# First and last batch of a fused attention and expert layer: filler turns, later weights, four output banks

## The reference

```
xn  = layernorm(x)
q, k, v = split(xn @ wqkv);  q, k = relu(q), relu(k);   16 heads of 16
kv  = cumsum(k[:, None] * v[None, :]);  y = (q . kv) / (q . cumsum(k) + 1e-5)
attention = y @ wo
scores = sigmoid(xn @ Wr);  the two best of 8 by scores + bias;  cw = their scores, normed
hid[e] = silu(xn @ Wg[e]) * (xn @ Wu[e]);  routed = sum over e < 4 of cw[e] * (hid[e] @ Wd[e])
routed += (cw[4] + cw[6]) * xn + cw[7] * relu(xn)
conv   = causal depthwise convolution of xn over 4 rows, + conv_b
out = x + attention + routed + conv
```

## Time and profile before

| | us |
|---|---|
| median of 3 runs | 1334.67 (1334.45 to 1334.83) |
| profiled execution, time | 1334.1 |
| its span, first to last instruction | 1332.3 |
| TensorE busy | 1312.0 |
| VectorE busy | 1120.6 |
| GpSimd busy | 822.7 |
| ScalarE busy | 737.4 |

### The profile page before, as it was taken

How to read it: one execution, slowest core, us unless ns; L and a number is a source line. 1 busy time by engine, 2 the same in 40 slices (tenths; PEclk the granted TensorE clock), 3 DMA queues, 4 the chain that set the end, 5 groups by cost and what they waited for, 6 DMA issues and landing times.

```text
span 1332.3 us, 54753 instructions
## 1 busy us (share of the span) xinstructions
PE 1312.0 (98%) x24384; PEld 1136.9 (85%) x24384; DVE 1120.6 (84%) x2574; ACT 737.4 (55%) x1543; POOL 822.7 (62%) x673
## 2 busy tenths in 40 slices
PE   5999999999999999999999999999999999999998
PEld 4888888888888888888888888888888888888887
DVE  7988889888898888898888988888888889888885
ACT  5645566545556455565555564556645655545561
POOL 2676566675575755666656757556666566575554
PEclk9999999999999999999999999999999999999999
DMA  5011211111211111111111011111111111111110
GB/s 181 30 39 66 66 53 47 35 66 66 66 34 50 51 66 65 50 50 35 66 66 65 35 49 51 66 66 50 50 34 67 66 65 35 35 65 50 51 49 18
DMA packets 46828, 73.73 MB, mean 55 GB/s; under 512 B 6529, under 2 KB 42241, under 8 KB 42497
## 3 DMA queue, kind: packets, MB, share of 16 engines
q1 hardware_dynamic: 45888, 69.23, 15.2%
q10 hardware_dynamic: 704, 1.01, 0.2%
HBM read 53.18 MB, written 17.04 MB: 53 GB/s over the span
## 4 chain that ended last, share of the span: by engine, by line
PE 97%; DVE 1%; POOL 0%; ACT 0%; DMA 0%; issue 0%; POOLq 0%; DVEq 0%
PE ring L303 51%; PE scores L303 17%; PE ring L423 7%; PE ring L439 6%; PE scores L372 5%; PE state_sum L386 4%; PE ring L459 2%; PE scores L312 2%; PE scores L354 2%; DMA x_t<-in_L_attn_x_dram 0%; DVE cT L828 0%; ACT qp L548 0%; DVE sm L807 0%; PE scores L321 0%; POOL hid L687 0%
## 5 line engine op out<-in xcount | busy, mean ns | idle before, releaser
L687 POOL TENSOR_TENSOR hid<-hid,cwb 128x512 f32<-128x512 f32 x128 | 172.0, 1343 | 225.4 <-DVE hid L836 224.7
L828 DVE SCALAR_TENSOR_TENSOR cT<-xT,conv_ws,cT 128x512 f32<-128x512 f32 x192 | 292.3, 1561 | 0.0
L675 POOL TENSOR_TENSOR x_t<-x_t,same 128x1024 f32<-128x1024 f32 x32 | 76.9, 2404 | 242.7 <-ACT same L557 242.7
L814 DVE TENSOR_TENSOR state_bd<-state_sum,tables_s 128x256 f32<-128x256 f32 x248 | 103.7, 418 | 135.9 <-PE state_sum L386 135.8
L578 ACT ACTIVATE sg<-ring 128x512 f32<-128x512 f32 x128 | 76.8, 600 | 251.3 <-PE ring L303 251.3
L303 PE MATMUL ring<-xl,wgu_h 128*128 128x512 f32 x512 | 212.3, 415 | 0.0
L691 POOL TENSOR_TENSOR hl<-hid,hh 128x512 fp32r<-128x512 f32 x128 | 208.4, 1628 | 0.0
L303 PE MATMUL ring<-xh,wgu_l 128*128 128x512 f32 x512 | 203.0, 396 | 0.0
L303 PE MATMUL ring<-xh,wgu_h 128*128 128x512 f32 x512 | 202.2, 395 | 0.0
L511 ACT ACTIVATE yh<-yT 128x256 fp32r<-128x256 f32 x128 | 53.5, 418 | 246.5 <-DVE yT L845 246.5
L807 DVE TENSOR_TENSOR sm<-scores,causal_s 128x512 f32<-128x512 f32 x256 | 158.5, 679 | 21.6 <-PE scores L372 21.6
(11 more groups left out here) (118 smaller groups left out, 3528.1 us busy)
## 6 DMA issues: line engine op xcount, KB each, us to landing
cwb<-cw_rows SPq DMA_DIRECT2D x32, 1024.0 KB, 4.7
x_t<-in_L_attn_x_dram SPq DMA_DIRECT2D x32, 512.0 KB, 4.4
out_dram<-x_t SPq DMA_DIRECT2D x31, 512.0 KB, 2.9
cw_rows<-cwt SPq DMA_DIRECT2D x128, 2.0 KB, 1.4
sm<-in_L_attn_wqkv_dram ACTq DMA_DIRECT2D x2, 384.0 KB, 5.0
sm<-in_L_ffn_Wg_dram SPq DMA_DIRECT2D x2, 256.0 KB, 3.5
sm<-in_L_ffn_Wu_dram SPq DMA_DIRECT2D x2, 256.0 KB, 4.6
cwb<-in_L_ffn_Wd_dram SPq DMA_DIRECT2D x1, 512.0 KB, 5.7
```

The costliest lines, as they stand in the source:

```text
L675: pool.tensor_tensor(xb, xb, same[:, :, :], ALU.add).then_inc(s_base1, 1)
L687: pool.tensor_tensor(hid[:, e, :], hid[:, e, :], cwb[:, e, :], ALU.mult).then_inc(s_hid, 1)
L814: dve.tensor_tensor(state_bd[:, n % 4, :].rearrange("p (g m n) -> p g m n", g=C, m=PPG), ST.unsqueeze(2).to_broadcast([P, C, PPG, BLK]), s ...
L828: ins = dve.scalar_tensor_tensor(out=cT[:, c, :], in0=xT[:, j % 2, c, n:n + BT], scalar=conv_ws[:, c, n:n + 1], in1=cT[:, c, :], op0=ALU.m ...
```

## The change

Three things change, all in the first and the last batch.

Start: TensorE turns the identity table into the bank `MID` 18 times before the first turns, 18 times after them and 20 times before the first scores (`keep_on`). VectorE makes `xl` straight from the turned x in PSUM, before it copies `xT`. The low parts of `wd` and `wo` are no longer made before the first batch, nor are the statistics and the normalised x of the second batch. `wd` is loaded into `hid[:, 2:4]` and `wo` into the place of the sequence's fourth batch in `x_t`, whose load is now issued behind both splits.

First batch: VectorE does the second batch's statistics and the low parts of `wd` and `wo` after `attend(1)`, in place of `tap(1)`; the taps come a tile later, two of them in tile 3. GpSimd normalises after `low_y(1)` and makes the second batch's low x after `weigh(3)`. TensorE turns the second batch's x after tile 2 instead of tile 1. ScalarE copies it after `high_y(2)` and makes its high part after `silu(3)`.

Last batch: `last_output` uses the four banks `SB` for the four output tiles; each expert's products go to all four tiles as soon as its low part is there, with turned convolution and attention between the third and the fourth expert.

```diff
-        st_o = st[:, 14 * D:16 * D].rearrange("p (c n) -> p c n", c=C)
-        st_d = cwb[:, 0:2, :].rearrange("p c n -> p (c n)").rearrange("p (e n) -> p e n", e=E)
+        st_d = hid[:, 2:4, :].rearrange("p c n -> p (c n)").rearrange("p (e n) -> p e n", e=E)
+        st_o = x_t[:, BPS - 1, 0:C, :]
...
+        N_FIRST = N_SPLITS - 2
...
-            for j in range(1, BPS):
+            for j in range(1, BPS - 1):
                 sp.dma_start(x_t[:, j], x_v[j]).then_inc(x_in[j], 16)
...
             spread_cw(0, 0, 0)
+
+            sp.wait_ge(w_split, N_SPLITS)
+            sp.dma_start(x_t[:, BPS - 1], x_v[BPS - 1]).then_inc(x_in[BPS - 1], 16)
             rounds(batch)
...
+            def keep_on(n):
+
+                for _ in range(n):
+                    nc.tensor.transpose(MID[:, 0:P], ident_s[:, :], ident_s[:, :])
...
                 if not k:
+                    pe.wait_ge(s_xT, C)
                     pe.wait_ge(w_split, EARLY)
...
+                def last_output():
+
+                    pe.wait_ge(s_sm, at(s, j, U * ROWS, U * ROWS))
+                    for e in range(E - 1):
+                        pe.wait_ge(s_hl, at(s, j, T, e + 1))
+                        for t in range(T):
+                            add_hidden(t, SB[t], e, first=e == 0)
+                    pe.wait_ge(s_conv, at(s, j, HALO, HALO))
+                    for t in range(T):
+                        turn_conv(t, SB[t], first=False)
+                        add_attention(t, SB[t])
+                    pe.wait_ge(s_hl, at(s, j, T, E))
+                    for t in range(T):
+                        add_hidden(t, SB[t], E - 1).then_inc(s_op, 1)
...
-                    if t == 1 and not last:
+
+                    if t == (2 if s == j == 0 else 1) and not last:
                         for c in range(C):
                             turn_xn(s, j, 1, c)
...
             pe.wait_ge(tables_in, 16)
+            keep_on(18)
             turn_first()
+            keep_on(18)
             pe.wait_ge(w_split, 2)
             heads(0, 0, 0)
+            keep_on(20)
             scores(0, 0, 0, 0)
...
-                if not last:
+                if not last and s + j:
                     fill_xT(s, j, 1)
                 silu(2)
-                if not last:
+                if not last and s + j:
                     high_x(s, j, 1)
                 high_hid(1)
                 high_y(2)
+                if s == j == 0:
+                    fill_xT(0, 0, 1)
                 silu(3)
+                if s == j == 0:
+                    high_x(0, 0, 1)
...
-                if not last:
+                if s == j == 0:
+                    normalise(0, 0, 1)
+                elif not last:
                     for c in range(C):
                         low_x(s, j, 1, c)
                 weigh(2)
                 low_hid(1)
                 low_y(2)
                 weigh(3)
+                if s == j == 0:
+                    for c in range(C):
+                        low_x(0, 0, 1, c)
...
             pool.wait_ge(set_up, 3)
             inverse_deviation(0, 0, 0)
-            normalise(0, 0, 1)
             base(0, 0, 0)
...
                     if t == 0:
                         mask(s, j, 0, 1)
+                    elif s == j == 0:
+
+                        if t == 1:
+                            statistics(0, 0, 1)
+                            low_weights(N_FIRST, N_SPLITS)
+
+                            dve.wait_ge(w_split, N_SPLITS)
+                        else:
+                            tap(t - 1)
+                        if t == T - 1:
+                            tap(t)
...
-            for c in (1, 0):
-                dve.wait_ge(s_xtr, C)
-                if c == 0:
-
-                    dve.wait_ge(s_xh, 1)
-                ins = dve.tensor_scalar(xT[:, 0, c, HALO:HALO + BT], XB[c][:, :], 1.0, None, ALU.mult)
-                ins.then_inc(s_xT, 1)
             for c in range(C):
-                dve.wait_ge(s_xT, C)
                 dve.wait_ge(s_xh, c + 1)
-                dve.tensor_tensor(xl[:, 0, c, :], xT[:, 0, c, HALO:HALO + BT], xh[:, 0, c, :].bitcast(F32),
+                dve.tensor_tensor(xl[:, 0, c, :], XB[c][:, :], xh[:, 0, c, :].bitcast(F32),
                                   ALU.subtract).then_inc(s_xl, 1)
-            low_weights(2, N_SPLITS)
+            for c in range(C):
+                dve.tensor_scalar(xT[:, 0, c, HALO:HALO + BT], XB[c][:, :], 1.0, None, ALU.mult).then_inc(s_xT, 1)
+            low_weights(2, N_FIRST)
...
-            statistics(0, 0, 1)
             router(0, 0, 0)
```

More of the change, by code:

```diff
@@ L447, in output @@
                         pe.wait_ge(s_out, at(s, j, T, T + 1))
-                    elif t == 0 or last:
-                        pe.wait_ge((s_y, s_gu, s_y)[t], at(s, j, T, T))
+                    elif t == 0:
+                        pe.wait_ge(s_y, at(s, j, T, T))
                     else:
                         pe.wait_ge(s_sig, at(s, j, T, T + 2 + t))
-                    late = last and t == 0
-                    def turn_conv():
-                        if t == 0:
-                            pe.wait_ge(s_conv, at(s, j, HALO, HALO))
-                        for c in range(C):
-                            mm(dst[:, c * P:(c + 1) * P], cT[:, c, ts], ident_s[:, :], is_transpose=True,
-                               start=c == 0 and not late, stop=False, skip_group_check=True)
@@ L462, in add_hidden @@
-                    def add_hidden():
-                        for e in range(E):
-                            if t == 0:
-                                pe.wait_ge(s_hl, at(s, j, T, e + 1))
-                            ins = product(dst[:, 0:D], [(hh[:, e, ts], hl[:, e, ts], wd_h[:, e, :], wd_l[:, e, :])],
-                                          first=late and e == 0, final=e == E - 1 and not late)
-                        return ins
-                    def add_attention():
-                        pe.wait_ge(s_yl, at(s, j, T, t + 1))
-                        return product(dst[:, 0:D], [(yh[:, c, ts], yl[:, c, ts], wo_h[:, c, :], wo_l[:, c, :])
-                                                     for c in range(C)], first=False, final=late)
@@ L817, in blocks, with low_weights @@
                                   .to_broadcast([P, C, PPG, BLK]), ALU.mult).then_inc(s_bd, 1)
+            def low_weights(first, stop):
+                for n in range(first, stop):
+                    _, _, hi, lo, src = SPLITS[n]
+                    dve.wait_ge(w_hi, n + 1)
+                    dve.tensor_tensor(lo, src, hi.bitcast(F32), ALU.subtract).then_inc(w_split, 1)
             def batch(s, j, left):
@@ L882, in batch @@
                     xb = x_t[:, j, t, :]
-                    dve.tensor_tensor(xb, OB[t][:, 0:D], xb, ALU.add).then_inc(s_out, 1)
-            def low_weights(first, stop):
-                for n in range(first, stop):
-                    _, _, hi, lo, src = SPLITS[n]
-                    dve.wait_ge(w_hi, n + 1)
-                    dve.tensor_tensor(lo, src, hi.bitcast(F32), ALU.subtract).then_inc(w_split, 1)
+                    done = SB[t] if last else OB[t]
+                    dve.tensor_tensor(xb, done[:, 0:D], xb, ALU.add).then_inc(s_out, 1)
             statistics(0, 0, 0)
```

45 lines of the change are left out of this document (30 added, 15 removed).

## The result

| | before | after |
|---|---|---|
| median of 5 runs, us | 1334.67 (1334.35 to 1334.83) | 1369.82 (1368.91 to 1372.39) |
| span of the profiled execution | 1332.3 | 1368.8 |
| TensorE busy | 1312.0 | 1328.9 |

What follows compares the result with a forecast made beforehand. TensorE was taken as the bound, busy 1312.0 of 1332.3 us. Start shift -3.75, tiles 2 and 3 +6.7, clock +1.7 and tail -4.8 summed to -0.15: 1334.5 us from a base of 1334.67, range 1331.0 to 1337.8.

Steps and rivals of the forecast that it cites:

- Step 1: Before the first batch: VectorE sets the pace, its shorter chain moves the first tile 3.75 us earlier; identity turns cost nothing.
- d: Shift of the whole first tile from VectorE's shorter chain before the first batch: -3.75 us (3.3 to 4.1 earlier).
- Step 2: First batch, tiles 1 and 2: late statistics and normalising make TensorE wait 0.8 us; gate and up of tile 3 start later.
- Step 3: First batch, tile 3: low x behind `weigh(3)` idles TensorE 4.6 us; second batch's value products start 2.95 us later.
- Step 4: After the stall before the second batch's value products: half clock on value and key products, +1.7 us (0.5 to 2.6).
- Step 5: Last batch: four output tiles at once leave TensorE no pause and keep its clock up, -4.8 us (-5.3 to -4.1).
- The sum: Whole kernel: start shift, tiles 2 and 3, clock and tail add to -0.15 us, giving 1334.5 us.
- rival (c): First batch: low x ends last, normalising late, value products +4.15 us, clock falls twice; 1337.4 us, chance 0.2.
- the milder row of hl: Trace row at 42.48 used for contention: a GpSimd operation of 1.26 to 1.3 us stretched to 1.74 by a tap.

Runs made afterwards that it cites:

- the padded one: The changed kernel with 36 tiny products (144 instructions) more ahead of its first turns, 256 extra with the change's own: 1338.46 us, ratio 1.0021.
- the one with low x first: The changed kernel with 256 instructions in front, second batch's low parts of x ahead of the fourth weighing on GpSimd instead of behind it: 1333.89 us, ratio 1.0003.

## Why the prediction was wrong

**Step 1, VectorE's prefix.** Sized right: the first mask stands at 27.54, d = -3.28 against -3.75, and 0.5 of that is the load of x, which landed 0.56 us later in this execution. But its other sentence is the step that failed: the identity turns, "I cost them at nothing". The price was sought on TensorE, within the waits that they fill. They were paid for in two other places: 29.6 us in the loop, by where the later code is cut (with 256 instructions in front instead of 112 it is 0.0), and some 3.5 us (1333.46 against 1329.98) that go, as far as the trace shows, through the other engines, which came to meet.

**Step 2, tiles 1 and 2.** The order was right, the sizes too small. The first gap (1.31 us, at 32.89) put VectorE's statistics at 40.02 instead of 38.25; power and normalising took 1.94 and 3.15 us instead of 1.12 and 2.24:

```profile
42.73 1.93 POOL L682 TENSOR_TENSOR rstd<-vare,half 128x4 f32<-128x4 f32 x1 [0.17 <-DVE vare L780]
...
46.38 1.52 POOL L688 TENSOR_SCALAR xn<-x_t,negm,rstd 128x256 f32<-128x256 f32 x1
...
46.23 1.41 DVE L865 SCALAR_TENSOR_TENSOR cT<-xT,conv_ws,cT 128x512 f32<-128x512 f32 x2
```

The power ran beside a low part of the weights (1.03 without it), and the fourth tile of xn, 0.56 us alone, until just after VectorE's taps. TensorE waited 1.4 and 2.1 us instead of 0.8 and fell to half clock. Gate and up of tile 3 started at 49.84, where 45.4 was forecast.

**Step 3, the stall before the value products.** The most exact term: 4.6 us forecast, 4.64 measured, with the forecast cause. What it was added to was 4.4 us late, so the start moved by +7.97 instead of +2.95.

**Step 4, the clock after it.** Right mechanism, too small: the shift grows from 7.97 at the value products to 10.5 at the keys' turns, so 2.5 us against 1.7 (its far bound was 2.6). The wait of 4.64 us came with 6.8 us at 1.2 GHz, 5.5 of them after it, against 3.4 us after the wait of 2.3 us in the kernel before.

**Step 5, the last batch.** -4.6 against -4.8. Right; alone, in the kernel before, the tail won 5.6 us in the medians of one job, 0.3 past the forecast's far bound.

**The sum.** Without the gaps the changed kernel takes 1338.5 us (the padded one), 2.9 over before in its job. Carried over to the forecast's base of 1334.67 that is 1337.6, close to rival (c) and just inside the range. That it comes so close is partly luck: (c) put 4.15 us on the start of the value products and 3.4 on the clock, and the padded kernel's products start 7.35 us late (59.00) and lose another 2.5; that execution, the slowest of the ten, was 5.2 us over the profiled one of before. The other 31 us no rival held: all were mechanisms of data and engines, and none asked whether a loop that is not touched can change. The earlier trace rows tempted to that: from 41.56 us on TensorE is never idle, which was read as a property of the loop. It was one of a loop at this place in the code.

## What to carry to other kernels

Count the instructions that a change adds in front of a long loop, on the engine that bounds it, also where they are free in time; then look in the trace after for "issue" inside a run of small products. If the gap's place goes back by a fixed number of products from batch to batch, try the same kernel with some tens of idle instructions more or fewer before judging the change: here 56, 112 and 168 in front of the kernel before gave +12, +32 and +20 us, and 256 in front of the changed one no loss in the loop. The tail's change moved no code ahead of it and cost the loop nothing (+0.09 us). And a faster start is no gain by itself; ask which two engines it brings together.

## What the runs showed of the hardware

**Code has a place.** TensorE lost 0.3 to 1.4 us where 128 small products with their loads took 2.2 to 2.5 us and a piece of its code ended there; the next piece took 2.6 to 3.9 us to come. With a transfer for every 256 instructions, a loop of 1545 a batch is always being loaded, and in the ten traces without a gap each transfer had landed at least 1.3 us before its piece was reached.

**VectorE waits out GpSimd's whole instruction.** Two products of VectorE with both operands in SBUF took 5.66 and 3.50 us beside long sums of GpSimd, 1.29 alone; once `base` waited they were 1.29 again. The prediction had gone by the milder row of hl, 1.74 instead of 1.26. The Trainium skill, "SBUF — State Buffer", section "SBUF: two separate sides", says that such instructions exclude each other for their full length; at these products the traces agree, and they show the price where GpSimd's instruction is 2.4 us long. Whether it also makes a kernel uneven is not shown: the one with low x first took from 1331.2 to 1339.8 us in ten runs of one program, and one of them was traced.

**Left open.** Why a transfer starts sometimes 0.3 and sometimes 1.5 us after TensorE has passed the same point, which sets whether a gap is 0.3 or 1.4 us; why the scores stay slow for 0.35 us after one; and whether the turns' last 3.5 us are the meeting of the two engines alone.
